# A transformer kernel on one core: the second cross attention joined to the block of self attention, and transposes half a step earlier

## The reference

```python
# layer 0: cross attention and feed forward (layernorm with weights ahead of each)
q = ln1(x) @ Wq                        # 16 heads of 32
k, v = ln2(ctx) @ Wkv
x = x + softmax(q k^T * scale) v @ Wproj + bproj
x = x + gelu(ln3(x) @ W1 + b1) @ W2 + b2
# layer 1: self attention, cross attention, feed forward
h = ln1(x); x = x + mha(h, h) @ sa_wo + sa_bo
h = ln2(x); x = x + mha(h, ctx) @ ca_wo + ca_bo
x = x + gelu(ln3(x) @ w1 + b1) @ w2 + b2
```

## Time and profile before

| what | value |
|---|---|
| median of 3 runs | 3306.97 us (3306.36 to 3311.73) |
| profiled execution: its own time | 3311.82 us |
| profiled execution: span | 3310.0 us |
| mean granted TensorE clock | 0.977 of full |
| TensorE busy | 3137.1 us (95%) |
| VectorE busy | 1806.8 us (55%) |
| ScalarE busy | 1570.9 us (47%) |
| GpSimd busy | 1329.1 us (40%) |
| self attention | about 1240 to 2167 us of the span |
| second cross attention | from about 2177 us |

### The profile page before, as it was taken

One profiled execution on the slowest core, in us unless ns is written; L12 is line 12 of the kernel. 1 busy time (PEld: TensorE's weight loads), 2 busy tenths in 40 slices (PEclk: granted clock), 3 DMA queues, 4 the chain that ended last, 5 costly groups with the idle time before them and its releaser, 6 DMA issues. The chain is left out here.

```text
span 3310.0 us, 41888 instructions
## 1 busy us (share of the span) xinstructions
PE 3137.1 (95%) x14480; PEld 2496.9 (75%) x14480; DVE 1806.8 (55%) x2848; ACT 1570.9 (47%) x2980; POOL 1329.1 (40%) x1355
## 2 busy tenths in 40 slices
PE   6599999999999998999999999859999999999999
PEld 5378877888888875777777777537888788888887
DVE  4588774322222336887888788758888432222221
ACT  2366663322222234777777777626666432222222
POOL 0345551333333216666666666735555111111110
PEclk8799999999999999999999999969999999999999
DMA  4423323211111123344344434332232411111100
GB/s 141 117 63 86 85 75 121 73 51 51 47 43 45 42 99 105 104 124 121 99 117 121 121 100 113 93 104 63 83 86 63 129 61 39 39 39 39 39 34 18
DMA packets 215046, 264.33 MB, mean 80 GB/s; under 512 B 78460, under 2 KB 100580, under 8 KB 214836
## 3 DMA queue, kind: packets, MB, share of 16 engines
q1 hardware_dynamic: 214835, 261.66, 26.7%
HBM read 125.12 MB, written 60.42 MB: 56 GB/s over the span
## 5 line engine op out<-in xcount | busy, mean ns | idle before, releaser
L1190 DVE TENSOR_REDUCE L1sa_nmax<-L1sa_s 128x2 f32<-128x1024 f32 x256 | 310.5, 1213 | 133.8 <-PE L1sa_s L1002 133.0
L1285 POOL TENSOR_TENSOR L1sa_El<-L1sa_E,L1sa_Eh 128x1024 fp32r<-128x1024 f32 x128 | 314.4, 2457 | 124.3 <-ACT L1sa_Eh L1108 124.3
L343 DVE TENSOR_TENSOR L1ff_gl<-L1ff_gf,L1ff_gh 128x512 fp32r<-128x512 f32 x128 | 95.9, 749 | 469.0 <-ACT L1ff_gh L327 469.0
L343 DVE TENSOR_TENSOR L0ff_gl<-L0ff_gf,L0ff_gh 128x512 fp32r<-128x512 f32 x128 | 96.2, 751 | 414.5 <-ACT L0ff_gh L327 414.5
L313 ACT ACTIVATE L1ff_gf<-L1ff_f,cols 128x512 f32<-128x512 f32 x128 | 88.3, 690 | 452.4 <-PE L1ff_f L101 452.4
L313 ACT ACTIVATE L0ff_gf<-L0ff_f,cols 128x512 f32<-128x512 f32 x128 | 88.3, 690 | 431.1 <-PE L0ff_f L101 431.0
L1115 ACT ACTIVATE L1sa_E<-L1sa_st 128x1024 f32<-128x1024 f32 x256 | 258.8, 1011 | 5.5 <-PE L1sa_st L1014 5.4
L99 PE MATMUL L0ff_acc<-L0ff_Wh,L0ff_gh 128*128 128x512 f32 x512 | 200.0, 391 | 6.8 <-DVE L0ff_gl L343 6.8
L99 PE MATMUL L0ff_f<-L0ca_hTh,L0ff_Wh 128*128 128x512 f32 x512 | 202.5, 396 | 0.0
L99 PE MATMUL L1ff_f<-L1ca_hTh,L1ff_Wh 128*128 128x512 f32 x512 | 202.1, 395 | 0.0
L1108 ACT ACTIVATE L1sa_Eh<-L1sa_E 128x1024 fp32r<-128x1024 f32 x192 | 200.6, 1045 | 0.2
(11 more groups left out here) (289 smaller groups left out, 8489.1 us busy)
## 6 DMA issues: line engine op xcount, KB each, us to landing
L1sa_OLN<-L1sa_osb SPq DMA_DIRECT2D x128, 192.0 KB, 2.7
L1sa_stack_q<-L1sa_parts_q SPq DMA_DIRECT2D x128, 128.0 KB, 2.6
L1sa_stack_k<-L1sa_parts_k SPq DMA_DIRECT2D x128, 128.0 KB, 2.6
L0ff_xs<-x SPq DMA_DIRECT2D x60, 256.0 KB, 2.9
L1ff_xs<-x SPq DMA_DIRECT2D x60, 256.0 KB, 3.6
L1ca_xs<-x SPq DMA_DIRECT2D x36, 256.0 KB, 3.0
L0ca_xs<-in_x SPq DMA_DIRECT2D x32, 256.0 KB, 3.1
L0ca_stage<-in_x SPq DMA_DIRECT2D x32, 256.0 KB, 2.8
```

Of the source, the lines that this page charges most:

```text
L343: nc.vector.tensor_tensor(gl[:, j % 2, :], gf[:, j % 2, :], f32(gh[:, j % 2, :]), ALU.subtract)\
L1190: nc.vector.reduce_max(nmax[:, h % 2, 2 * (n % 2):2 * (n % 2) + 2], s_bank[:, :, :], AX.X, negate=True)\
L1285: nc.gpsimd.tensor_tensor(El[:, n % 2, :], E[:, n % 3, :], f32(Eh[:, n % 2, :]), ALU.subtract)\
```

## The change

1. The second cross attention and feed forward (L1ca, L1ff) are built into the block of L0ca, L0ff and L1sa. They take the semaphores of L0ca and L0ff and count on from where those ended; the tiles' places in SBUF are rearranged. There is one barrier less.
2. The first parts of L1ca are made in self attention's last batch, by a table of its steps (`CA_AHEAD`, of 32): loads at step 10, statistics 12 to 15, rsqrt 16, normalising 17 to 20, transposes 21 to 24, halves of wq 26 and 27, zeros between 20 and 26, and at step 28 the 14 DMAs that place keys and values (`first_keys`).
3. For the last 12 pairs all Eh are ScalarE's and all El VectorE's (`LAST_PAIRS`).
4. Of self attention's last products with wo, quarters 0 to 2 come first, into banks `st` and `o`, then two query products and three score tiles of L1ca and a third query product, then quarter 3.
5. In both cross attentions' leads: statistics and normalising of batch 1 stand in front of maximum 1 and 2, the third query product behind score tile 1, the halves of wo move to halves 9 and 12 of batch 0, the zeros are eight memsets of which six precede the rsqrt.
6. `T_HALVES` is (2, 3, 4, 5) instead of (3, 4, 5, 6), `FF_OVER_OUTPUT` 4 instead of 6, and the feed forward's first weights wait for the last transposes.
7. The eight DMAs that stack the first group's k are issued by ScalarE.

The diff, cut to its core:

```diff
-    def events(self, name, per=1, unit=1, skip=0):
-        self.sems.append(self.nc.alloc_semaphore(f"{self.name}_{name}"))
-        return Count(self.sems[-1], per, unit, skip)
+    def events(self, name, per=1, unit=1, skip=0, batches=None):
+        if self.earlier is None:
+            self.sems.append(self.nc.alloc_semaphore(f"{self.name}_{name}"))
+            self.counts[name] = Count(self.sems[-1], per, unit, skip, batches)
+        else:
+            before = self.earlier.counts[name]
+            self.counts[name] = Count(before.sem, per, unit, skip, batches, before.end)
+        return self.counts[name]
...
-    EH_BY = ("act", "act", "act", "act", "act", "pool", "act", "pool")
-    EL_BY = ("pool", "dve", "pool", "dve", "pool", "dve", "pool", "dve")
+    EH_BY = ("act", "act", "act", "act", "act", "pool", "act", "pool") * (PAIRS // 8)
+    EL_BY = ("pool", "dve", "pool", "dve", "pool", "dve", "pool", "dve") * (PAIRS // 8)
+    EH_BY, EL_BY = EH_BY[:-LAST_PAIRS] + LAST_PAIRS * ("act",), EL_BY[:-LAST_PAIRS] + LAST_PAIRS * ("dve",)
 
...
+    def last_products(pe, quarters):
+        wh, wl = W["wo"]
+        for c in quarters:
+            if c == 0:
+                pe.wait_ge(e_ex.sem, e_ex.no(PAIRS - 1))
+            pe.wait_ge(e_ol.sem, e_ol.no(GROUPS - G + c))
+            for t in range(TT):
+                ts = slice(t * P, (t + 1) * P)
+                if c == 0 and t >= 2:
+                    pe.wait_ge(e_ob.sem, e_ob.no(HEADS - TT + t))
+                last = product(nc, last_bank(t), oTh[:, c, ts], oTl[:, c, ts], wh[:, c, :], wl[:, c, :],
+                               c == 0, c == KT - 1)
+                if c == KT - 1:
+                    last.then_inc(e_unit.sem, e_unit.unit)
...
+    def last_residual(dve, t):
+        dve.wait_ge(rx_full[t % 2].sem, rx_full[t % 2].no(((B - 1) * TT + t) // 2))
+        dve.wait_ge(e_unit.sem, e_unit.no(len(units) + t))
+        nc.vector.tensor_tensor(residual(B - 1, t), last_bank(t), residual(B - 1, t), ALU.add)\
+            .then_inc(e_res.sem, e_res.unit)
...
+                    for pair in range(2):
+                        stacks(act, "k", 0, pair)
...
+                    if b == B - 1 and n % STEPS in CA_AHEAD.transposes:
+                        if n % STEPS == CA_AHEAD.transposes[0]:
+                            evacuated(pe, len(units) - 2)
+                            evacuated(pe, len(units) - 1)
+                        ca.T(pe, 0, CA_AHEAD.transposes.index(n % STEPS))
...
+            last_products(pe, range(KT - 1))
+            ca.first_products(pe)
...
-T_HALVES = (3, 4, 5, 6)
+T_HALVES = (2, 3, 4, 5)
+FIRST_STATS, FIRST_NORMS = 0, 2
+CA_AHEAD = Names()
+CA_AHEAD.load, CA_AHEAD.stats, CA_AHEAD.norms = 10, (12, 13, 14, 15), (17, 18, 19, 20)
+CA_AHEAD.transposes, CA_AHEAD.weights = (21, 22, 23, 24), (26, 27)
+CA_AHEAD.zeros, CA_AHEAD.keys = (20, 21, 23, 24, 25, 26), 28
+LAST_PAIRS = 12
+WO_HALVES = (9, 12)
...
+    def first_loads(sp):
+        if sa is not None:
+            sp.wait_ge(sa.e_unit.sem, sa.keys_done)
+        for t in range(TT):
+            load(sp, 0, t)
+        load_weights(sp, wt, 0, WQ)
...
+    def first_keys(sp):
+        sp.wait_ge(e_zero.sem, e_zero.no(5))
+        place_k(sp, 0)
+        place_v(sp, 0)
+        place_k(sp, 1)
...
+    def zeros(pool, i):
+        if sa is not None and i == 0:
+            pool.wait_ge(sa.e_unit.sem, sa.keys_done)
+        if sa is not None and i == 2:
+            pool.wait_ge(sa.e_vst.sem, sa.values_placed)
+        if sa is not None and i == 6:
+            pool.wait_ge(sa.e_unit.sem, sa.units_done)
+        part = slice(i % 2 * G, (i % 2 + 1) * G)
+        at = Kb[:, (i - 2) // 2, part, :, :] if 2 <= i < 6 else Vb[:, i // 6, :, part, :]
+        nc.gpsimd.memset(f32(at), 0.0).then_inc(e_zero.sem, e_zero.unit)
...
+    def first_products(pe):
+        pe.wait_ge(wt.lo.sem, wt.lo.no(WQ - 1))
+        for kind, b, i in CA_FIRST[:2]:
+            for c in range(KT):
+                piece(pe, kind, b, i, c)
...
+            if sa is None:
+                first_loads(sp)
+                first_keys(sp)
+                load_weights(sp, wt, WQ, WO)
+                second_loads(sp)
+            else:
+                second_loads(sp)
+                sa.last_residuals(sp)
+            if sa is not None:
+                sp.wait_ge(sa.e_unit.sem, sa.units_done)
+                load_weights(sp, wt, WQ, WO)
+                sa.last_stores(sp)
...
+                if s == 2:
+                    for kind, b, i in CA_FIRST[2:]:
+                        for c in range(KT):
+                            piece(pe, kind, b, i, c)
+                if s == 3 and sa is not None:
+                    sa.last_products(pe, [KT - 1])
...
+                if s == 1 and sa is not None:
+                    sa.last_high(act)
...
+                if s == FIRST_NORMS:
+                    for t in range(TT):
+                        normalise(dve, 1, t)
...
+                if s == 1 and sa is not None:
+                    sa.last_low(dve)
+                if s == FIRST_STATS:
+                    for t in range(TT):
+                        stat(dve, 1, t)
+                    aggregate(dve, 1)
+                if s in (3, LEAD - 1) and sa is not None:
+                    for t in range(2):
+                        sa.last_residual(dve, 2 * (s == LEAD - 1) + t)
...
+            if sa is None:
+                for i in range(6):
+                    zeros(pool, i)
+                rsqrt(pool, 0)
+                for c in range(KT):
+                    lo(pool, 0, c)
...
+        sa_main(ca2)
+        ca2_main(ff2)
+        ff2_main()
```

841 lines of the change are left out of this document (434 added, 407 removed).

## The result

| | median | runs |
|---|---|---|
| before | 3306.66 us | 4, 3305.97 to 3311.73 |
| changed | 3286.97 us | 4, 3286.56 to 3288.92 |

The ratio is 0.9933, 95% interval 0.9921 to 0.9945: the changed kernel is faster by 19.7 us (0.6%). The forecast was a gain of 42 us, to 3265 (3249 to 3284). The result lies 22 us above the forecast and 3 us outside its range. It lies nearest to rival B (3280, the last batch stretches), which had a chance of 0.15.

The account below looks back on a forecast made before the run. TensorE, 95% busy, bounds the kernel, so only its standing time can be won. Seam 30, first cross attention's start 8 and self attention's start 4 sum to 42 us: 3307.0 to 3265 us, range 3249 to 3284.

Parts of the forecast that it names:

- rival B: Self attention's last batch stretches with VectorE the chain throughout: T0 15 to 20 us later, 3280 us; chance 0.15.
- Against it stands T0 itself: Self attention's last batch: VectorE's added work makes T0 come 7 us later, bounds 1 and 12.
- T0: Mark where products with wo follow self attention's last product; 2152.28 us before the change, expected near 2147.
- By the row I charge nothing beyond the 7 us: Last batch: VectorE's contention with GpSimd, judged from low halves of E (median 1.22, longest 1.96 us), adds nothing.
- the term that was feared most: Last 12 pairs: VectorE gets six more low halves of E at 1.22 us, 7.3 us.
- The seam from T0 to tile 6: Between self attention and second cross attention: 77.2 us before, 38.3 us summed for the changed kernel.
- tile 6: Mark: exponentials of the first cross attention tile behind the lead, 2229.45 us at the seam before the change.
- the forecast chain of 9.0 us: At the seam, from the query high half through maximum, statistics and exponentials to o's last low half: 9.0 us.
- The bias load: Second cross attention: GpSimd waits for the load behind SP's last stores, costing 2 us, bounds 0 and 5.
- The first cross attention's start: Earlier rsqrt and a shorter lead before tile 6's exponentials: 8 us gained, 5 to 9.
- Self attention's start: k's DMAs issued from ScalarE's queue let the first scores start earlier: 4 us gained, 0 to 6.
- At nothing: Parts given no gain: transposes one half earlier in 16 batches, feed forward's weights, counting on semaphores, new SBUF places.

Follow-up runs that it names:

- loads_spread: Changed kernel with the second block's six loads issued one a step instead of all in one step of the last batch; median 3284.74 us.
- pairs_0: Changed kernel with none of the last 12 pairs' halves of E moved (high to ScalarE, low to VectorE); median 3286.42 us.
- pairs_6: Changed kernel with the halves of E moved in the last 6 pairs instead of the last 12; median 3286.46 us.
- add_up: Changed kernel with loads spread, key and value DMAs late, bias load early, casts of h on ScalarE, wq's conversion behind the last pair; 3272.62 us.
- wq_load_late: add_up with the two query weight loads issued at steps 24 and 26 instead of 14 and 15; median 3273.04 us.
- keys_late: Changed kernel with the 14 DMAs for keys and values issued behind head 127's line-up, as before the change; median 3281.68 us.
- bias_early: Changed kernel with the second cross attention's output bias load issued ahead of SP's last stores; median 3282.07 us.
- halves_back: Changed kernel with the next batch's transposes at half steps 3 to 6 again, in both layers; median 3288.72 us.

## Why the prediction came out wrong

**The step that failed is "Against it stands T0 itself": 7 us, bounds 1 to 12.** It measured 16.7 to 18.4 over the two profiles of either kernel. The prediction counted VectorE's room over two long stretches, 15 us against 15 to 17 us of work. Windows of the changed kernel (columns as above) show what came of it:

```profile
2108.00:2118.00 10.00, 4.99 (x20) 2.67 (x18) 9.89 (x7) 6.46 (x10) 6.42 (x6) 0.98 0.08 31
2118.00:2128.00 10.00, 9.66 (x29) 5.54 (x29) 10.00 (x11) 7.69 (x11) 4.93 (x6) 0.68 0.22 66
2128.00:2138.00 10.00, 7.48 (x39) 4.88 (x37) 8.61 (x9) 9.02 (x13) 8.80 (x10) 1.00 0.14 42
2138.00:2148.00 10.00, 5.07 (x12) 2.28 (x12) 10.00 (x7) 5.62 (x8) 8.55 (x7) 0.68 0.00 1
```

VectorE is busy 38.5 of these 40 us, which is rival B's picture ("VectorE over 95% busy"), and B's 15 to 20 us for T0 came true; in the last twelve pairs alone it is less (29.2 of 32 us from 2123 to 2155). TensorE's longest waits in it, and ScalarE's one:

```profile
2116.84 0.73 PE L1038 MATMUL L1sa_s<-L1sa_stack_k,L1sa_stack_q 96*128 96x512 f32 x2 [3.25 <-DVE L1sa_nmax L1216]
...
2146.58 1.17 PE L1083 MATMUL L1sa_o<-L1sa_El,L1sa_Vst 128*96 128x512 f32 x2 [3.07 <-DVE L1sa_El L1224]
2150.13 1.19 PE L1050 MATMUL L1sa_st<-L1sa_stack_q,L1sa_stack_k 98*128 98x512 f32 x2 [2.38 <-ACT L1sa_E L1145]
```

```profile
2147.69 0.72 ACT L873 ACTIVATE L1sa_onorm<-L1sa_onorm,cols 128x512 f32<-128x512 f32 x1 [4.38 <-POOL L1sa_onorm L1338]
```

The last three hang together on VectorE: the cast at 2141.66 (2.13 us) stands in front of a reciprocal (to 2145.44). The low half of E comes behind that, and GpSimd's normalising waits for it, then ScalarE's bias, then its exponentials.

What the runs show of the 17 us (T0 in one profile of each, with the change of the median):
- The burst of six loads: 5.9 us of T0, 2 in the median (loads_spread). The prediction counted what the moved loads free at the seam but not what they push aside where they land: SP's queue at step 10, with the small DMA of row maxima behind it. This lies ahead of the two stretches that it looked at, which begin at 2106.5 in the kernel before. Its list of VectorE's new work also leaves out the four statistics of 0.68 us; what they cost was not tried.
- The casts and normalisings at their length beside GpSimd. Casts off VectorE: 2.7 us (2 in the median); normalisings left out: 2.2 us (3). The list took the casts at 0.5 to 1.2 us each and "By the row I charge nothing beyond the 7 us"; they took 0.41, 0.76, 2.33 and 2.13. It took the normalisings at 2.28 together; they took 3.5. The low halves of wq, taken at 2.87, took 3.52. With 7.3 us for E that makes 19.9 us for 15 us of room.
- The weights' conversion: 0.7 to 1.5 us, within the spread.

"By the row" meant the low halves of E, a subtraction that reads two tiles. The trace of the kernel before has rows of the right kind: the same cast beside GpSimd, and the normalising (shortest, median and longest in ns).

```profile
2193.23 1.20 DVE L239 CAST L1ca_hTh<-L1ca_htmp 128x512 fp32r<-128x512 f32 x1 [0.42 <-ACT L1ca_htmp L234]
```

```profile
2192.89 1.26 POOL L243 TENSOR_TENSOR L1ca_hTl<-L1ca_htmp,L1ca_hTh 128x512 fp32r<-128x512 f32 x1 [4.54 <-DVE L1ca_hTh L239]
```

```profile
L394 DVE TENSOR_SCALAR L0ff_stage<-L0ff_xs,L0ff_mv,L0ff_rs x30: 535/542/1514, 622.9 to 1265.0; 128x512 f32<-128x512 f32 x30
```

The cast took 1.20 us there instead of 0.43, and ended 0.28 us after GpSimd's instruction. So the contention itself could be read before the run, if not its length in the last batch.

Against that, the term that was feared most, six more low halves of E, is neutral by itself (pairs_0, pairs_6).

Of add_up's T0, 905.3, which is still 9.7 us behind before's 895.6, 2.2 are the normalisings. The 16 transposes moved into the batch take TensorE 2.4 us there (four times 0.60); that these lengthen it one for one was not tried. Some 5 us stay open. The transfer of the weights is not it (wq_load_late).

**The seam from T0 to tile 6**: 38.3 forecast, 39.2 and 38.9 measured, with one wait of 2.67 for osb127 (3.5 forecast), one of 4.57 for the low half of o (the forecast chain of 9.0 us took 8.7) and none over 5 us. The sum was right, by small errors that stand against each other. The first 36 products took 10.1 us without the wait (8.4 forecast), as seven of them ran at 0.63 us each, and the last 12 took 5.3 (4 forecast), all but the first at 0.63. The wait, the chain and the tail were 0.8, 0.3 and 0.8 shorter. keys_late shows that the wait with what follows from it was worth 5.4 us.

**The mark was put at nothing.** 77.2 − 38.3 takes it that both kernels have done the same work at tile 6. The changed one has some 20 instructions of TensorE more behind it, 2.3 to 2.7 us.

**The bias load**: 2 us forecast, bounds 0 and 5. The stretch behind tile 6 is 4.8 us longer, but by the windows above only 1.2 to 2.1 of that is standing time, and bias_early takes 2.3 off the standing time. GpSimd waited 6.52 us for the load. The mechanism was right and the size about right.

**The first cross attention's start**: 8 us forecast, 5 to 9. Tile 6 came 9.7 us earlier (153.5 to 143.8), but feed forward only 6.7 earlier (4.6 between the second profiles, just outside the bounds). The 3 us between the marks are work that now stands behind tile 6, 3.7 to 5.0 us; TensorE's standing time there is shorter, by 0.7 to 2.0 us.

**Self attention's start**: 4 us forecast, 3.0 measured. Of these 2.2 are the issuing queue, as argued.

**At nothing**: the transposes one half earlier were put at nothing or a gain within the first term; they bring 2 us over both layers in the median, and 3 to 5 by the marks of the slowest execution of halves_back.

By the marks: +6.7 +3.0 −16.7 +38.0 −4.8 = 26.2 us from the profile of before at 3304.5 (last product) to 3278.8, which is 25.7. The medians differ by 19.7 to 23.7, as before's first profile ran 4.9 us above its median. Forecast on the same basis: +8 +4 −7 +38.9 −2 = 42. Of the 16 us between them 9.7 are T0, 2.8 the stretch behind tile 6, and the other three 0.9 to 1.3 each.

No run parts the barrier that is gone from the first parts moved ahead (parts 1 and 2 of the change); the gain at the seam is that of both.

## What to carry to other kernels

Work that is moved into a full loop must be laid against the windows of that loop step by step, on each engine and on the issuing queue, not against its mean idle time: here 38 us won at the seam cost 17 in the batch, and five small changes of place won 14 us more. Spread a burst of loads over the steps, and look which small DMA stands behind it. Where ScalarE has room, put a cast that is new beside a busy GpSimd there, and price it from a row that has the same kind of instruction in the same company, or keep its range wide. Before you subtract two stretches, count whether both kernels have done the same work at the marks.

## What the runs showed of the hardware

- VectorE's cast and tensor_scalar of 128x512 took 0.41 and 0.54 us with GpSimd idle and up to 2.33 and 1.73 us beside it (changed kernel, 2136.61 and 2121.65), ending 0.28 us after GpSimd's memset, which only writes; a low half of E (128x1024, two inputs, at 2129.42) took its 1.21 us though zeros on GpSimd overlapped it (1.39 from 2128.62).
- A DMA share of 0.94 at 258 GB/s over 10 us (loads_spread) went with TensorE 9.43 us busy. Behind six loads issued at once (2 MB) a stack of 128 KB took 6.3 us to land instead of 2.6, and TensorE stood 4.77 us.
- A short wait cost more than its length: after the wait of 2.67 us at 2164.55 the products of wo went from 0.39 us each to 0.63 for some 3 us, at a granted clock of 0.50 (the level of 1.2 GHz; window below), then back to 0.39 at a clock of 1.00.

```profile
2165.70:2168.60 2.90, 2.90 (x8) 2.34 (x7) 1.34 (x1) 0.00 (x0) 1.27 (x1) 0.50 0.90 278
```
